# Graph network on one core: filter input on ScalarE's queue, ScalarE compares for four tiles, aggregation by source half

## The chip, the cores and the metric

One core of a Trainium2 chip. The metric is device time in microseconds of one execution.

## What is computed

256 nodes with 512 features, 4352 edges sorted by target. Two residual layers on x:

```python
# layer 0: normalised dense adjacency, applied to a linear map
h = relu(layernorm(x))
adj[src, dst] = 1; adj[dst, src] = 1; adj += eye
adj = adj * dinv[:, None] * dinv[None, :]          # dinv = deg ** -0.5
x = x + adj @ (h @ W0) + bias0
# layer 1: edge filters, gather, tensor products, scatter
h = relu(layernorm(x))
hs, hv = h[:, :128] @ w_in2f_s, h[:, 128:] @ w_in2f_v      # 32 channels, scalar and 3-vector
s, v = hs[dst], hv[dst]
Wf = (softplus_shifted(edge_attr_20 @ W1 + b1) @ W2 + b2) * edge_weight
edge = products of s, v, edge_attr_4 and Wf
agg = segment_sum(edge, src)
x = x + output_net(agg)
```

(dst and src stand here in the roles of idx_j and idx_i; only the products that reach the output are needed.)

## The kernel before

The 4352 edges are 34 tiles of 128; a group is four tiles, so there are nine groups (the last of two tiles). Every engine has its own program, and the order in each is written out by hand; semaphores join them.

Compares. VectorE builds one-hot matrices Os and Od [128 edges, 256 nodes] in bf16 for each tile, in seven waves (WAVES, function onehots, line 406): an is_equal of iota_r with the edges' ids for Os and another for Od. Od lies in the memory of WQ, which gets its own data later (so rows on line 412 call it WQ). TensorE counts the edges between nodes with Os and Od (adjacency, line 601) into banks 4 and 5, and from that VectorE makes CI (line 454), TensorE transposes it (line 666, called CT here) and VectorE makes A and the degrees (line 465), degve (line 469) and GpSimd the two scales by a power (line 354, scales(1) first).

Layer 0. VectorE does the statistics of x (lines 431 to 437) and h1, TensorE transposes h1 (line 625), ScalarE copies the result out (h1T, line 214), and TensorE multiplies by W0 in four k blocks for each half of the nodes (first_layer, line 629). The product is scaled and split into two parts, hW_hi on ScalarE (line 251) and hW_lo on VectorE (line 479). A times these gives L0 (line 674), in the order hi of both halves, then lo of both. x1 (line 485) is L0 times dinv plus xb, where xb = x + bias0 (line 472, VectorE).

Filter net. TensorE makes z from the filter input f_sb and w1 (hidden, line 611, three pieces). ScalarE takes Abs of each (line 207), then Exp (218) and Ln (221) of all, VectorE adds the positive part into za (line 446), ScalarE rounds hX and hY (231, 232), VectorE takes the rests hXlo (449) and hYlo (475). The output weights are split into w2_hi (ScalarE, 216) and w2_lo (VectorE, 442), the bias row into b2p on GpSimd (lines 341 to 347). filters(g) (line 636) multiplies group by group.

Layer 1. After x1 come h2, its transposes (line 688) and node channels (695), which end in HL (277, 504). Node one-hots OdT [128 nodes, 4352 edges], two halves of the nodes (a = 0, 1) and four chunks of the edges, are compares with dst_bc: on VectorE (node_onehots, line 459) chunks 0 and 1 of both halves, on GpSimd (node_onehots_late, line 358) chunks 3 and 2 of half 0, on ScalarE (lines 244 and 247) chunks 2 and 3 of half 1, as 1 minus distance. The loop over the groups (gather 721, VectorE 514 to 565, ScalarE 301, 305, 240, 284, 268, GpSimd 378, 395, 399, scatter 733) and the tail follow.

Loads. SP's queue issues idx, x, f, w0, dst, bias0, then small ones; ScalarE's queue w1, w2, b2, yr. xb lies in the memory of f_sb.

## Time and profile before

| | |
|---|---|
| median of 3 runs | 71.96 us (71.57, 71.96, 72.97) |
| profiled execution | 71.83 us, its span 69.8 us |
| TensorE matmul busy | 61.7 us (88%), granted clock 0.988 of full |
| VectorE busy | 60.1 us (86%) |
| ScalarE busy | 48.6 us (70%) |
| GpSimd busy | 39.5 us (57%) |
| DMA | 5.65 MB, nearly all of the loads before 16.5 us |

All times below are microseconds from the start of the span. An engine that is not busy for a moment matters only where something on the last chain waits for it.

### The profile page before, as it was taken

Reading aid. Unit: us, or ns where it says so; the run is one execution under the profiler, and the core shown is the slowest. Engines: PE = TensorE matmul, PEld = TensorE weight load, DVE = VectorE, ACT = ScalarE, POOL = GpSimd, SP = SyncE. Lnnn points to the kernel's source line nnn. Section 1 sums busy time; section 2 is a strip of 40 time slices with the busy share of each in tenths; the row PEclk is TensorE's granted clock in tenths of the full one; section 3 lists DMA queues with packets and bytes.
Section 4 is the critical chain, followed back from the end, with each engine's and each line's share of the span. In section 5 each row is a group of like instructions: output and inputs, shape, how many; then the busy total and the mean of one; then the engine's idle time right before and its main releaser. Section 6 shows DMA issues by size and latency. Waiting matters only on the chain.

```text
span 69.8 us, 1215 instructions
## 1 busy us (share of the span) xinstructions
PE 61.7 (88%) x407; PEld 48.6 (70%) x407; DVE 60.1 (86%) x124; ACT 48.6 (70%) x74; POOL 39.5 (57%) x46
## 2 busy tenths in 40 slices
PE   3999998999999999897998979999999999998340
PEld 1236754568834268796987969998898989997220
DVE  4599999999979968989999898989898999972760
ACT  0700059978999697967979999988696969732700
POOL 5000030000676989594799979999999988700000
PEclk9999999999999999999999999999999999999995
DMA  0899998984000000000000000000000000000044
GB/s 1 129 396 247 361 499 379 449 317 124 9 0 0 0 0 0 0 0 5 0 0 0 0 0 9 5 0 0 0 0 0 0 0 9 0 0 0 0 148 153
DMA packets 3049, 5.65 MB, mean 81 GB/s; under 512 B 540, under 2 KB 1936, under 8 KB 2916
## 3 DMA queue, kind: packets, MB, share of 16 engines
q1 hardware_dynamic: 2274, 5.14, 21.3%
q10 hardware_dynamic: 770, 0.44, 2.2%
q8 instruction: 3, 0.05, 0.3%
q14 instruction: 2, 0.02, 0.1%
HBM read 5.06 MB, written 0.52 MB: 80 GB/s over the span
## 4 chain that ended last, share of the span: by engine, by line
DVE 45%; PE 20%; issue 14%; ACT 13%; DMA 3%; DVEq 0%; ACTq 0%
ACT OsR L240 8%; DVE WQ L412 7%; DVE Os L412 7%; PE pair L632 5%; ACT w_sb L284 5%; DVE dst_bc L565 4%; PE pair L733 4%; PE pair L742 4%; DVE pair L514 3%; PE pair L674 3%; DMA idx_sb<-idx 3%; PE pair L721 3%; DVE w_sb L485 2%; DVE za L446 2%; DVE hX L449 2%
## 5 line engine op out<-in xcount | busy, mean ns | idle before, releaser
L733 PE MATMUL pair<-OsR,Mh 128*128 128x256 f32 x56 | 13.6, 281 | 0.0
L733 PE MATMUL pair<-OsR,Ml 128*128 128x256 f32 x56 | 13.6, 281 | 0.0
L721 PE MATMUL pair<-HL,OdT 128*128 128x256 f32 x68 | 10.1, 289 | 1.6 <-DVE dst_bc L565 0.7
L395 POOL TENSOR_TENSOR Ml<-dst_bc,Mh 128x512 fp32r<-128x512 f32 x8 | 10.4, 1305 | 1.1 <-ACT Mh L301 1.0
L721 PEld LDWEIGHTS pair<-HL,OdT 128*128 128x128 f32 x68 | 8.6, 188 | 2.8 <-issue 2.8
L733 PEld LDWEIGHTS pair<-OsR,Ml 128*128 128x128 f32 x56 | 10.5, 188 | 0.0
L733 PEld LDWEIGHTS pair<-OsR,Mh 128*128 128x128 f32 x56 | 10.5, 188 | 0.0
L605 PEld LDWEIGHTS pair<-WQ,Os 128*128 128x128 bf16 x68 | 6.8, 104 | 4.0 <-DVE WQ L412 1.8
L605 PE MATMUL pair<-WQ,Os 128*128 128x256 bf16 x68 | 9.4, 297 | 0.2 <-DVE WQ L412 0.2
L399 POOL TENSOR_TENSOR Ml<-dst_bc,Mh 128x512 fp32r<-128x512 f32 x7 | 9.2, 1309 | 0.0
L240 ACT ACTIVATE OsR<-Os 128x1024 fp32r<-128x1024 bf16 (+1 forms) x9 | 9.0, 999 | 0.0
L632 PE MATMUL pair<-w_sb,h1T 128*128 128x512 f32 x16 | 7.7, 601 | 0.3 <-ACT h1T L214 0.3
L305 ACT ACTIVATE Mh<-dst_bc 128x512 fp32r<-128x512 f32 (+1 forms) x9 | 5.5, 609 | 3.1 <-DVE dst_bc L565 3.0
L514 DVE TENSOR_TENSOR pair<-pair,w_sb 128x512 f32<-128x512 f32 (+1 forms) x10 | 6.2, 619 | 1.3 <-ACT w_sb L284 1.2
L358 POOL TENSOR_SCALAR OdT<-dst_bc,iota_c 128x1088 fp32r<-128x1088 int32 x2 | 6.1, 3054 | 1.6 <-DVE OdT L459 1.4
L341 POOL CAST b2p<-b_sb 96x128 bf16<-96x128 f32 x1 | 1.4, 1402 | 8.3 <-issue 8.3
L534 DVE TENSOR_TENSOR pair<-pair,WQ 128x512 f32<-128x512 f32 (+1 forms) x9 | 6.0, 662 | 0.1
L378 POOL TENSOR_TENSOR WQ<-WQ,y 128x256 f32<-128x256 f32 (+1 forms) x9 | 5.8, 652 | 0.1
L207 ACT ACTIVATE za<-pair 128x512 f32<-128x512 f32 (+1 forms) x3 | 1.4, 489 | 6.3 <-PE pair L613 6.3
L284 ACT ACTIVATE w_sb<-pair 128x512 f32<-128x512 f32 (+1 forms) x10 | 5.2, 518 | 0.8 <-PE pair L721 0.7
L412 DVE TENSOR_TENSOR Os<-iota_r,idp 128x512 bf16<-128x512 bf16 (+3 forms) x7 | 5.6, 796 | 0.0
L412 DVE TENSOR_TENSOR WQ<-iota_r,idp 128x512 bf16<-128x512 bf16 (+3 forms) x7 | 5.6, 796 | 0.0
(122 smaller groups left out, 140.2 us busy)
## 6 DMA issues: line engine op xcount, KB each, us to landing
dst_bc<-dst_row SPq DMA_DIRECT2D x1, 2176.0 KB, 12.9
w_sb<-w SPq DMA_DIRECT2D x1, 1024.0 KB, 8.1
x_sb<-x SPq DMA_DIRECT2D x1, 512.0 KB, 4.4
out<-x_sb SPq DMA_DIRECT2D x2, 192.0 KB, 1.9
f_sb<-f_t SPq DMA_DIRECT2D x1, 378.0 KB
b_sb<-bias SPq DMA_DIRECT2D x1, 256.0 KB, 13.1
w_sb<-w ACTq DMA_DIRECT2D x1, 128.0 KB, 4.1
out<-x_sb ACTq DMA_DIRECT2D x1, 128.0 KB, 1.9
```

Of the source, the lines that this page charges most:

```text
L240: nc.scalar.activation(OsR[:, g % RG, 0:n, :], Os[:, t0:t0 + n, :], ACT.Copy).then_inc(q["OsR"], 1)
L284: nc.scalar.activation(G_lo[:, g % RS, j0:j1, :, :], rows_of(g)[:, j0:j1, 1, :, :], ACT.Copy).then_inc(q["Glo"], 1)
L358: nc.gpsimd.tensor_scalar(OdT[:, 0, c * E // 4:(c + 1) * E // 4], dst_bc[:, c * E // 4:(c + 1) * E // 4], iota_c[:, 0:1], None, ALU.is_equ ...
L395: nc.gpsimd.tensor_tensor(Ml[:, o, 0:n, feats(1)], M[:, o, 0:n, feats(1)], Mh[:, o, 0:n, feats(1)].bitcast(fp32), ALU.subtract).then_inc(q ...
L399: nc.gpsimd.tensor_tensor(Ml[:, o, 0:n, feats(0)], M[:, o, 0:n, feats(0)], Mh[:, o, 0:n, feats(0)].bitcast(fp32), ALU.subtract).then_inc(q ...
L412: last = nc.vector.tensor_tensor(into[:, t0:t1, :].rearrange("p t (h k) -> p t h k", k=2), nodes, of_edge, ALU.is_equal)
L514: nc.vector.tensor_tensor(hi, hi, G_lo[:, g % RS, j0:j1, :, :].rearrange("p t c f -> p t (c f)"), ALU.add).then_inc(q["add"], 1)
L534: nc.vector.tensor_tensor(L, G, wq[:, :, 3:7, :], ALU.mult).then_inc(q["Q"], 1)
L605: last = nc.tensor.matmul(bank[4 + a][:, 0:N], Os[:, t, a * P:(a + 1) * P], Od[:, t, :], start=(t == 0), stop=(t == T - 1))
L632: last = nc.tensor.matmul(bank[a][:, :], h1T[:, a, k, :], w0_sb[:, k, :], start=(k == 0), stop=(k == KD - 1))
L721: last = nc.tensor.matmul(gpair[g % 2][:, j * 2 * C:(j + 1) * 2 * C], OdT[:, a, t * P:(t + 1) * P], HL[:, a, :, :], start=(a == 0), stop=( ...
L733: last = nc.tensor.matmul(bank[4 + b][:, 0:N], part[:, g % RG, j, feats(b)], OsR[:, g % RG, j, :], start=(TG * g + j == 0 and part is Mh), ...
```

## The change

- The filter input f_t is loaded first on ScalarE's queue instead of third on SP's. The hidden products are put between the adjacency products of early waves; the waves become (0,2) (2,4) (4,8) (8,12) (12,20) (20,28) (28,30).
- The one-hots of tiles 30 to 33 are made on ScalarE: eight Abs of iota_r minus the id (negidx) and two Relu of one minus the distance. Their adjacency products stand between the transposes of the two halves of h1.
- b2p is made of two parts in fp32r instead of three in bf16: a copy on ScalarE, a difference on GpSimd.
- xb moves from VectorE to GpSimd, ahead of scales. hYlo is done in three pieces. w2_lo goes behind the last wave.
- Node one-hots: ScalarE keeps chunk 2 of half 1, VectorE takes chunk 3 of half 1 and does chunk 0 of half 0 between the two hW_lo; GpSimd does chunk 2, then 3, of half 0. The scratch of ScalarE's (gap) lies in h1.
- A times hW goes by half: hi and lo of half 0, then of half 1. One k block of the second half of the first layer goes ahead of CT.
- y_blocks(0, free) goes ahead of ScalarE's node one-hot, wc_sb's copy ahead of h2.

```diff
     WARM = 6
-    WAVES = ((0, 2), (2, 6), (6, 12), (12, 20), (20, 28), (28, 32), (32, T))
+    TA = 4
+    TV = T - TA
+    WAVES = ((0, 2), (2, 4), (4, 8), (8, 12), (12, 20), (20, 28), (28, TV))
     LN_EPS = 1e-5
...
             sp.dma_start(x_sb[:, :, :], x.rearrange("(a p) d -> p a d", p=P)).then_inc(d_x, 16)
-            sp.dma_start(f_sb[0:KF, :], f_t).then_inc(d_f, 16)
             sp.dma_start(w0_sb[:, :, :], w0.rearrange("(k p) n -> p k n", p=P)).then_inc(d_w0, 16)
...
+            act.dma_start(f_sb[0:KF, :], f_t).then_inc(d_f, 16)
             act.dma_start(w1_sb[:], w1).then_inc(d_w1, 16)
...
+            act.wait_ge(d_idx, 16)
+            nc.scalar.activation(negidx[:, :, :], idx_sb[:, :].rearrange("p (h t) -> p h t", h=2)[:, :, TV:T], ACT.Copy,
+                                 scale=-1.0).then_inc(q["negidx"], 1)
+            act.wait_ge(q["negidx"], 1)
+            act.wait_ge(q["iota"], 1)
+            act.wait_ge(q["half"], 3)
+            for h, into in enumerate((Os, Od)):
+                for i in range(TA):
+                    nc.scalar.activation(dist[:, h, i, :], iota_r[:], ACT.Abs, bias=negidx[:, h, i:i + 1]).then_inc(q["dist"], 1)
+                act.wait_ge(q["dist"], TA * (h + 1))
+                nc.scalar.activation(into[:, TV:T, :], dist[:, h, :, :], ACT.Relu, bias=one[:, 0:1],
+                                     scale=-1.0).then_inc(q["near"], 1)
             absolute(0)
...
                 nc.scalar.activation(h1T[:, a, :, :], bank[(6, 1)[a]][:, :], ACT.Copy).then_inc(q["h1T"], 1)
+            act.wait_ge(d_b2, 16)
+            nc.scalar.activation(b2p[:], b2_sb[:], ACT.Copy).then_inc(q["b2p"], 1)
             act.wait_ge(d_w2, 16)
...
                 t0, n = TG * g, tiles(g)
-                act.wait_ge(q["onehot"], wave(t0 + n - 1))
+                act.wait_ge(q["onehot"], wave(min(t0 + n, TV) - 1))
+                if t0 + n > TV:
+                    act.wait_ge(q["near"], 2)
                 if g >= RG:
...
-            act.wait_ge(d_dst, 16)
-            act.wait_ge(q["negc"], 1)
-            nc.scalar.activation(gap, dst_bc[:, E // 2:], ACT.Abs, bias=iota_n[:, 1:2]).then_inc(q["gap"], 1)
-            act.wait_ge(q["gap"], 1)
-            act.wait_ge(q["half"], 3)
-            nc.scalar.activation(OdT[:, 1, E // 2:], gap, ACT.Relu, bias=one[:, 0:1], scale=-1.0).then_inc(q["OdTa"], 1)
-            act.wait_ge(q["scales"], 1)
-            for a in range(NH):
-                act.wait_ge(q["hW"], a + 1)
-                nc.scalar.activation(hW_hi[:, a, :], bank[a][:, :], ACT.Copy, scale=s1[:, a:a + 1]).then_inc(q["hW_hi"], 1)
-            act.wait_ge(q["OdTa"], 1)
+            act.wait_ge(q["near"], 2)
             act.wait_ge(q["adj"], 1)
...
             y_blocks(0, free)
+            act.wait_ge(d_dst, 16)
+            act.wait_ge(q["negc"], 1)
+            act.wait_ge(q["tp1"], NH)
+            nc.scalar.activation(gap, dst_bc[:, E // 2:3 * E // 4], ACT.Abs, bias=iota_n[:, 1:2]).then_inc(q["gap"], 1)
+            act.wait_ge(q["scales"], 1)
+            for a in range(NH):
+                act.wait_ge(q["hW"], a + 1)
+                nc.scalar.activation(hW_hi[:, a, :], bank[a][:, :], ACT.Copy, scale=s1[:, a:a + 1]).then_inc(q["hW_hi"], 1)
+            act.wait_ge(q["gap"], 1)
+            nc.scalar.activation(OdT[:, 1, E // 2:3 * E // 4], gap, ACT.Relu, bias=one[:, 0:1],
+                                 scale=-1.0).then_inc(q["OdTa"], 1)
+            act.wait_ge(q["wc"], 1)
+            nc.scalar.activation(wc_sb[:], bank[1][:, 0:B], ACT.Copy, scale=SF * SB).then_inc(q["wcs"], 1)
+            act.wait_ge(q["OdTa"], 1)
             act.wait_ge(q["x1"], 1)
...
                 filters_out(g)
-            act.wait_ge(q["wc"], 1)
-            nc.scalar.activation(wc_sb[:], bank[1][:, 0:B], ACT.Copy, scale=SF * SB).then_inc(q["wcs"], 1)
             act.wait_ge(q["s2"], 1)
...
             nc.gpsimd.memset(one[:], 1.0).then_inc(q["half"], 1)
-            nc.gpsimd.memset(ones[:], 1.0).then_inc(q["ones"], 1)
+            nc.gpsimd.memset(ones[:].bitcast(i32), 0x3f800000).then_inc(q["ones"], 1)
...
-            pool.wait_ge(q["onehot"], len(WAVES))
-            pool.wait_ge(d_b2, 16)
-            nc.gpsimd.tensor_copy(b2p[:], b2_sb[:]).then_inc(q["b2p"], 1)
             pool.wait_ge(q["b2p"], 1)
-            nc.gpsimd.tensor_tensor(b2r[:], b2_sb[0:64, :], b2p[0:64, :], ALU.subtract).then_inc(q["b2r"], 1)
-            pool.wait_ge(q["b2r"], 1)
-            nc.gpsimd.tensor_copy(b2p[0:64, :], b2r[:]).then_inc(q["b2p"], 1)
+            nc.gpsimd.tensor_tensor(b2p[32:64, :], b2_sb[32:64, :], b2p[32:64, :].bitcast(fp32), ALU.subtract).then_inc(q["b2p"], 1)
             pool.wait_ge(q["b2p"], 2)
-            nc.gpsimd.tensor_tensor(b2p[0:32, :], b2r[0:32, :], b2p[0:32, :], ALU.subtract).then_inc(q["b2p"], 1)
-            pool.wait_ge(q["b2p"], 3)
+            pool.wait_ge(d_x, 16)
+            pool.wait_ge(d_b0, 16)
+            pool.wait_ge(q["z"], 3)
+            nc.gpsimd.tensor_tensor(xb[:, :, :], x_sb[:, :, :], b0_sb[:].unsqueeze(1).broadcast_to((P, NH, D)),
+                                    ALU.add).then_inc(q["xb"], 1)
             pool.wait_ge(q["degve"], 1)
...
             pool.wait_ge(q["scales"], 2)
-            node_onehots_late(3)
+            node_onehots_late(2)
             pool.wait_ge(q["OdTp"], 1)
...
             scaled_late(1)
-            pool.wait_ge(q["OdT"], 4)
-            node_onehots_late(2)
+            node_onehots_late(3)
             scaled_late(2)
...
             onehots(2)
+            onehots(3)
...
             nc.vector.tensor_scalar(ve[:], mv1[:, :, 1], LN_EPS, None, ALU.add).then_inc(q["ve"], 1)
-            for w in range(3, len(WAVES)):
+            for w in range(4, len(WAVES)):
                 onehots(w)
-                if w == 4:
-                    dve.wait_ge(q["w2hi"], 1)
-                    nc.vector.tensor_tensor(w2_lo[:], w2_sb[:], w2_hi[:].bitcast(fp32), ALU.subtract).then_inc(q["w2lo"], 1)
+                if w == 5:
                     dve.wait_ge(q["zln"], 1)
...
                                                        ALU.max, ALU.add).then_inc(q["hT"], 1)
+            dve.wait_ge(q["w2hi"], 1)
+            nc.vector.tensor_tensor(w2_lo[:], w2_sb[:], w2_hi[:].bitcast(fp32), ALU.subtract).then_inc(q["w2lo"], 1)
             dve.wait_ge(q["hhi"], 1)
...
-            dve.wait_ge(d_b0, 16)
-            nc.vector.tensor_tensor(xb[:, :, :], x_sb[:, :, :], b0_sb[:].unsqueeze(1).broadcast_to((P, NH, D)),
-                                    ALU.add).then_inc(q["xb"], 1)
             dve.wait_ge(q["hhi"], 2)
-            nc.vector.tensor_tensor(hY[0:64, :], za[64:128, :], hY[64:128, :].bitcast(fp32), ALU.subtract).then_inc(q["hYlo"], 1)
+            for c in range(3):
+                cols = slice(c * NG * P // 3, (c + 1) * NG * P // 3)
+                nc.vector.tensor_tensor(hY[0:64, cols], za[64:128, cols], hY[64:128, cols].bitcast(fp32),
+                                        ALU.subtract).then_inc(q["hYlo"], 1)
             dve.wait_ge(q["scales"], 1)
+            dve.wait_ge(d_dst, 16)
             for a in range(NH):
...
                                                hW_hi[:, a, :].bitcast(fp32), ALU.mult, ALU.subtract).then_inc(q["hW_lo"], 1)
+                if a == 0:
+                    node_onehots(0, 0)
             dve.wait_ge(q["scales"], 2)
...
             dve.wait_ge(q["x1"], 2)
+            dve.wait_ge(q["OdTa"], 1)
             nc.vector.tensor_scalar(h2[:, 1, :], x1[:, 1, :], float(D), xsum[:, 1:2], ALU.mult,
...
                                     ALU.max).then_inc(q["h2T"], 1)
-            dve.wait_ge(d_dst, 16)
-            for a in range(NH):
-                node_onehots(a, 0)
+            node_onehots(1, 0)
+            node_onehots(0, 1)
             dve.wait_ge(q["s2"], 1)
...
                                                HL[:, a, 0, :].bitcast(fp32), ALU.mult, ALU.subtract).then_inc(q["Hl"], 1)
-            for a in range(NH):
-                node_onehots(a, 1)
+            node_onehots(1, 1)
+            node_onehots(1, 3)
...
                     dve.wait_ge(q["OdT"], 4)
-                    dve.wait_ge(q["OdTp"], 2)
+                    dve.wait_ge(q["OdTp"], 1)
+                    dve.wait_ge(q["OdTa"], 1)
                 dve.wait_ge(q["add"], g + 2)
...
                 for t in ts:
-                    pe.wait_ge(q["onehot"], wave(t))
+                    if t < TV:
+                        pe.wait_ge(q["onehot"], wave(t))
+                    else:
+                        pe.wait_ge(q["near"], 2)
                     for a in range(NH):
                         last = nc.tensor.matmul(bank[4 + a][:, 0:N], Os[:, t, a * P:(a + 1) * P], Od[:, t, :],
-                                                start=(t == 0), stop=(t == T - 1))
-                if t == T - 1:
+                                                start=(t == 0), stop=(t == TV - 1))
+                if t == TV - 1:
                     last.then_inc(q["adj"], 1)
...
-            adjacency(range(2, 6))
-            adjacency(range(6, 12))
-            pe.wait_ge(d_f, 16)
-            pe.wait_ge(d_w1, 16)
-            for c in range(3):
-                hidden(c)
-            pe.wait_ge(q["eye"], NH + 1)
-            for a in range(NH):
+            def transposed(a):
+                pe.wait_ge(q["eye"], NH + 1)
                 pe.wait_ge(q["h1"], a + 1)
...
                 last.then_inc(q["tp1"], 1)
+            adjacency(range(2, 4))
+            pe.wait_ge(d_f, 16)
+            pe.wait_ge(d_w1, 16)
+            hidden(0)
+            hidden(1)
+            adjacency(range(4, 8))
+            hidden(2)
+            adjacency(range(8, 12))
+            transposed(0)
+            adjacency(range(TV, T))
+            transposed(1)
             pe.wait_ge(d_w0, 16)
...
             first_layer(0, 2, 3)
-            adjacency(range(20, T))
+            adjacency(range(20, TV))
             first_layer(0, 3, KD)
+            first_layer(1, 0, 1)
...
             last.then_inc(q["CT"], 1)
-            first_layer(1, 0, KD)
-            for p, (part, ready) in enumerate(((hW_hi, "hW_hi"), (hW_lo, "hW_lo"))):
-                for b in range(NH):
+            first_layer(1, 1, KD)
+            for b in range(NH):
+                for p, (part, ready) in enumerate(((hW_hi, "hW_hi"), (hW_lo, "hW_lo"))):
                     pe.wait_ge(q[ready], b + 1)
...
```

## Rows read from the trace of the kernel before

**Rows 1.** The page, chain that ended last, by engine.
```profile
DVE 45%; PE 20%; issue 14%; ACT 13%; DMA 3%; DVEq 0%; ACTq 0%
```
**Rows 2.** Timeline, VectorE: start us, us, engine, line, operation, count, idle before.
```profile
2.76 0.23 DVE L423 CAST idp<-idx_sb 128x136 bf16<-128x136 int32 x1 [0.71 <-DMA idx_sb<-idx]
...
9.32 0.38 DVE L437 TENSOR_SCALAR ve<-mv 128x2 f32<-128x2 f32 x1
9.62 1.21 DVE L412 TENSOR_TENSOR Os<-iota_r,idp 128x2048 bf16<-128x2048 bf16 x1
...
14.16 0.41 DVE L442 TENSOR_TENSOR w_lo<-w_sb,w_hi 128x256 fp32r<-128x256 f32 x1
14.49 1.47 DVE L446 SCALAR_TENSOR_TENSOR za<-pair,za 128x512 f32<-128x512 f32 x3
...
17.87 1.35 DVE L449 TENSOR_TENSOR hX<-za,hX 64x1152 fp32r<-64x1152 f32 x1
19.25 0.76 DVE L454 SCALAR_TENSOR_TENSOR warmup<-pair,eye_sb 128x256 bf16<-128x256 f32 x2
...
21.31 0.16 DVE L469 TENSOR_TENSOR deg<-deg,ve 128x2 f32<-128x2 f32 x1
21.39 1.22 DVE L472 TENSOR_TENSOR f_sb<-x_sb,b_sb 128x1024 f32<-128x1024 f32 x1
...
24.03 1.44 DVE L479 SCALAR_TENSOR_TENSOR hW_lo<-pair,scales,hW_hi 128x512 fp32r<-128x512 f32 x2
26.31 0.75 DVE L485 SCALAR_TENSOR_TENSOR w_sb<-pair,scales,f_sb 128x512 f32<-128x512 f32 x1 [0.84 <-PE pair L674]
...
29.71 1.47 DVE L459 TENSOR_SCALAR OdT<-dst_bc,iota_c 128x1088 fp32r<-128x1088 int32 x2
```
**Rows 3.** Timeline, ScalarE.
```profile
10.68 1.08 ACT L214 ACTIVATE h1T<-pair 128x512 f32<-128x512 f32 x2
11.65 0.42 ACT L216 ACTIVATE w_hi<-w_sb 128x256 fp32r<-128x256 f32 x1
...
13.15 1.25 ACT L221 ACTIVATE za<-za,warm 128x1152 f32<-128x1152 f32 x1
...
23.22 1.46 ACT L251 ACTIVATE hW_hi<-pair,scales 128x512 fp32r<-128x512 f32 x2 [0.60 <-POOL scales L354]
```
**Rows 4.** Timeline, TensorE matmuls (CT is line 666).
```profile
8.10 2.10 PE L613 MATMUL pair<-f_sb,w_sb 84*128 84x512 f32 x6
10.04 1.04 PE L625 MATMUL pair<-id_sb,h 128*128 128x128 f32 x8
11.42 1.95 PE L632 MATMUL pair<-w_sb,h1T 128*128 128x512 f32 x4 [0.34 <-ACT h1T L214]
13.21 1.91 PE L605 MATMUL pair<-WQ,Os 128*128 128x256 bf16 x16
...
20.07 0.40 PE L666 MATMUL pair<-eye_sb,warmup 128*128 128x128 bf16 x4 [0.17 <-DVE warmup L454]
```
**Rows 5.** Timeline, GpSimd (y, b2p, the first scales).
```profile
9.05 0.62 POOL L335 TENSOR_TENSOR y<-yr_sb 128x136 f32<-128x136 f32 x1 [7.54 <-DMA yr_sb<-yr]
17.97 1.40 POOL L341 CAST b2p<-b_sb 96x128 bf16<-96x128 f32 x1 [8.29 <-issue]
...
21.61 1.58 POOL L354 TENSOR_TENSOR scales<-deg,neghalf 128x2 f32<-128x2 f32 x1 [0.89 <-POOL b2p L347]
```
**Rows 6.** The page, costliest groups: busy us, mean ns, idle before.
```profile
L395 POOL TENSOR_TENSOR Ml<-dst_bc,Mh 128x512 fp32r<-128x512 f32 x8 | 10.4, 1305 | 1.1 <-ACT Mh L301 1.0
```
**Rows 7.** The bias row's load: its issue in SP's timeline, and its landing time.
```profile
3.15 0.44 SPq L184 DMA_DIRECT2D b_sb<-bias  x1
b_sb<-bias SPq DMA_DIRECT2D x1, 256.0 KB, 13.1
```
**Rows 8.** Windows: PE, PEld, DVE, ACT, POOL busy, PEclk, DMA share, GB/s.
```profile
0.00:5.60 5.60, 4.26 (x13) 1.60 (x14) 3.83 (x11) 1.28 (x1) 0.88 (x10) 1.00 0.67 182
37.10:56.50 19.40, 18.30 (x145) 17.32 (x144) 18.20 (x38) 17.16 (x28) 18.77 (x20) 1.00 0.00 1
```

34 lines of the change are left out of this document (19 added, 15 removed).

## The prediction

> **What bounds the kernel now.** I read the page first (busy shares, then the chain that ended last), then the chain in order of time, then the timeline of each engine up to 37 us, and last the DMA issues. VectorE has the largest part of the chain, 45% [rows 1]. The span has three stretches. From 0 to about 26 us the graph is prepared: compares, adjacency, first layer, aggregation. From 26 to 37 us come the second norm and the filters. From 37 us nine groups of edges run through a loop. Six passes take the 19.4 us of one window, 3.2 each, with VectorE busy for 18.2 and ScalarE for 17.2 of it [rows 8]. The diff leaves every instruction of the loop and of the tail in place, so I carry both over unchanged. What counts is when x1 (line 485) starts, now at 26.31 [rows 2]: all behind it follows from it, and the sum is a sum of shifts of that one moment.
>
> Up to there two engines share the limit. VectorE has no gap of note from 2.76 to 20.0 [rows 2]. TensorE is held by compares until the hidden products start at 8.10 and has almost no break from there to the transposes of CI (CT) at 20.07 [rows 4].
>
> **The change, part by part.**
> *Filter input first.* idx, x, the filter input f (378 KB) and w1 are 0.97 MB together. Up to 5.6 us the DMA engines moved 182 GB/s, which is 1.02 MB [rows 8]. So I let f and w1 be there at 5.6 (bounds 5.0 and 6.2). The hidden products stood at 8.10; TensorE gets work for its early gap.
>
> *TensorE up to the transposes of h1.* From 5.6: hidden products 1.94 in all (8.10 to 10.04), three blocks of eight adjacency products at 0.88 (16 take 1.91 with the last one's run-out, so 0.11 each), transposes 0.9. That ends at 5.6 + 5.5 = 11.1. Before it was 11.08 [rows 4]. The early start is spent, because the products of the four ScalarE tiles now stand ahead of the second transposes.
>
> *ScalarE.* Eight Abs of 256 elements, at most 0.42 each as w2_hi took, two casts of 1024 at about 1.0 and three Abs of z (1.4) fill 3.4 to at most 10.6, where ScalarE was mostly idle. Then comes a queue that nothing hides: second h1T copy at 11.2, 0.5; b2p copy 0.2 (new here); w2_hi, Exp and Ln 2.75 (11.65 to 14.40) [rows 3]. Ln ends at 14.7 instead of 14.40.
>
> *VectorE.* Four tiles fewer save 8 x 0.14 = 1.1 us (a compare of eight tiles takes 1.21), the extra early wave adds 0.14, and w2_lo (0.33) goes behind. VectorE would reach za (line 446) at 14.3, but za waits for Ln: 14.75 to 16.15, before 14.49 to 15.89. The last wave is now two tiles (2 x 0.33), then w2_lo 0.33, then hXlo, which waits for ScalarE's hX: 17.4. Left alone, hXlo would run 17.45 to 18.8 and CI (line 454) start at 18.83, 0.4 sooner than 19.25 [rows 2]. TensorE agrees: from 11.1, two k blocks 1.79 (11.42 to 13.21), 16 products 1.75, a block 0.87, 20 products 2.2, two blocks 1.74 give 19.45; CT comes at 19.65, behind CI, in place of 20.07 [rows 4].
>
> *xb moves to GpSimd (line 472).* This is the term that decides. VectorE took 1.22 us for it. On GpSimd the nearest row is a tensor_tensor of 512 fp32 elements, 1.305 us [rows 6], so 2.6 for 1024. It waits for the bias row, which lands at 3.15 + 13.1 = 16.25 [rows 7], and it reads SBUF, as do VectorE's instructions of just that time: the last wave, w2_lo and hXlo have two SBUF operands each. The trace shows that such pairs exclude each other. GpSimd's cast b2p took 1.40 us, from 17.97 to 19.37, for 128 elements, while VectorE's hX ran 17.87 to 19.22 [rows 2, 5]. The first scales took 1.58 for two elements beside VectorE's xb, which ended at 22.61. The other way round, VectorE's ve (line 437, two elements) took 0.38 where degve took 0.16, and ended at 9.70, just after GpSimd's y at 9.67. So I take full exclusion: GpSimd gets in at 16.25 or at the next instruction's end (16.5), mean 16.35, and keeps VectorE's two-operand work out until 18.95. Then the rest of the last wave 0.45 on average, w2_lo 0.33, hXlo 1.37: CI at 21.1, 1.85 later than before. The other bound is no exclusion: CI at 18.83.
>
> The Trainium skill says the same of this pair ("SBUF — State Buffer", Who interferes with whom): a VectorE instruction with two SBUF inputs contends with a GpSimd instruction that reads SBUF, and whoever starts first keeps the shared ports for the whole instruction. The rows above agree, but in none of them does a long GpSimd instruction hold VectorE.
>
> *From CI to x1.* CI to the end of degve takes 2.2 (19.25 to 21.47), as before. Then the move pays. The first scales ended 1.7 after degve because xb stood in front; now only a third of hYlo (0.5) does, and it is ready after 1.1. hW_hi and hW_lo are 0.7 each [rows 2, 3]. Between the two hW_lo stands a node one-hot of 0.7 (two take 1.47). The second hW_hi is ready 0.7 after the first, so the one-hot costs its 0.7 in front of the second hW_lo, which is the last that x1 waits for. Exclusion case: degve ends 23.3, scales 24.4, first hW_hi 25.1, first hW_lo 25.8, one-hot 26.5, second hW_lo 27.2, x1 0.55 later (two products): 27.75, +1.45. Without exclusion: 21.05, 22.15, 22.9, 23.6, 24.35, 25.1, x1 25.7: -0.6. In both, TensorE's first layer (CT + 3.0: 24.9 or 22.65) is just in time. The order by source half is worth nothing by itself, as the last wait is the second hW_lo in both orders.
>
> *The rest, at nothing.* ScalarE's node one-hots halve, and VectorE gains a chunk but does chunk (0,0) ahead of x1, so from x1 to the first rows_sum it has four chunks in both kernels. The wc copy goes ahead of h2, into idle time of ScalarE; without that cover it costs 0.3. GpSimd's late one-hot need not wait for OdT and GpSimd starts its loop 1 to 2 us sooner, but the loop does not wait for it. The bias product in 64 rows of fp32r streams as many columns; if its weight load is slower it shows 0.1 before the transposes of h2.
>
> **Sum.** Profiled execution 71.83 (span 69.8 and 2.0 around it) + 1.45 = 73.3. That execution stands 0.13 below the median of 71.96; I make no correction.
>
> **The rivals.**
> *1. No exclusion, or GpSimd yields between pieces.* For it: no row shows a long GpSimd instruction holding VectorE, and ve is a tiny case. Against: the pairs above that met did exclude. 71.83 - 0.6 = 71.2, faster than before. It decides when VectorE is held for less than about 0.8 us.
> *2. idx comes late.* Its load has been beside w1 (rows of 512 B); now it is beside the 4.6 KB rows of f. VectorE's start at 2.76 hangs on it [rows 2]. Up to 0.4 is absorbed, as za waits for Ln anyhow. If it is 1.4 late and nothing excludes: 71.2 + 1.0 = 72.2; with exclusion the two overlap in part, about 73.8. The Trainium skill has each DMA engine take turns between queues packet by packet ("DMA: Bandwidth & Descriptors", Queues, rings and completion order). No row here shows what a large packet does to a small one beside it.
> *3. More gain than I see.* f at 5.0 takes 0.4 off Ln; then VectorE limits, za at 14.3, x1 at 25.2; without exclusion 70.7. To pass 2% (70.5) the loop would have to gain as well.
>
> **Chances and range.** Exclusion 0.50, no exclusion 0.30, idx late 0.10, more gain 0.10. About 2% (1.4 us) is what a measurement of this kernel can tell from no change. The exclusion case straddles that bound: 0.28 of its 0.50 goes to slower, the rest to within. idx late gives 0.04 to slower, more gain 0.08 to faster. So faster 0.08, within 0.60, slower 0.32. The likeliest case has 72.7 to 73.9 as its own range (the bias row or GpSimd 0.6 sooner at best, 0.6 of idx on top at worst). With both signs the range is 70.9 to 73.9.
>
> **What the profile after would show.** xb on GpSimd near 16.3 to 19 and the last wave or hXlo on VectorE stretched or ending late, near 21: forecast right. hXlo ending near 18.8 beside a running xb: rival 1. idp starting after 3.2: rival 2. Hidden products at about 5.6, Ln ending near 14.7, scales 1.1 after degve, the second hW_lo as the last release of x1, and six loop passes in 19.3 us test the other steps. The prediction is wrong if the bias row lands after 17.5 (xb would then lie beside CI and A, which read PSUM), or if the loop's period moves: 0.1 there is 0.8 in the end.

## The result: 78.5 us, 7% slower

| | before | changed |
|---|---|---|
| median | 71.79 us (4 runs, 71.57 to 72.97) | 78.48 us (4 runs, 76.62 to 79.91) |
| profiled execution, its span | 71.83, 69.8 us | 79.89, 77.8 us |
| TensorE's mean granted clock | 0.988 | 0.920 |

The ratio is 1.072, interval 1.069 to 1.076. The forecast was 73.3, range 70.9 to 73.9: it is wrong, outside the range. In some executions of the changed kernel TensorE's clock is low for one or two stretches; the ratio leaves them out, and the profile below is of one with two such stretches.

The page of the changed kernel: the rows of TensorE and of its granted clock over 40 slices, then the chain that ended last, by engine and by line.

```profile
PE   3909999999999976989999999999999999998630
...
PEclk9998555899999999999758999999999999999995
...
PE 64%; DVE 13%; ACT 7%; DMA 5%; issue 5%; POOL 1%; DVEq 0%
PE pair L769 17%; PE pair L757 13%; PE pair L684 8%; PE pair L631 6%; DMA idx_sb<-idx 5%; PE pair L681 5%; PE pair L639 5%; PE pair L778 3%; PE pair L728 2%; DVE za L463 2%; DVE hW_lo L499 2%; ACT za L238 2%; DVE OdT L478 2%; ACT hX L248 2%; POOL scales L373 1%
```

In place of VectorE with 45% [rows 1], TensorE has 64% of the chain. Four of the entries were not among the fifteen largest before: the filter products (L684), the adjacency products (L631), the bias product (L681) and the hidden products (L639). The load of idx has gone from 3% to 5%. The clock row has a hole at about 8 to 14 us and another at 38 to 41.

VectorE's timeline of the changed kernel up to x1 (start, length, line, operation, idle before it and its releaser):

```profile
4.86 0.23 DVE L441 CAST idp<-idx_sb 128x136 bf16<-128x136 int32 x1 [2.81 <-DMA idx_sb<-idx]
...
19.52 1.49 DVE L463 SCALAR_TENSOR_TENSOR za<-pair,za 128x512 f32<-128x512 f32 x3 [3.27 <-ACT za L238]
...
23.62 0.76 DVE L473 SCALAR_TENSOR_TENSOR warmup<-pair,eye_sb 128x256 bf16<-128x256 f32 x2
...
25.68 0.16 DVE L488 TENSOR_TENSOR deg<-deg,ve 128x2 f32<-128x2 f32 x1
...
27.89 0.75 DVE L499 SCALAR_TENSOR_TENSOR hW_lo<-pair,scales,hW_hi 128x512 fp32r<-128x512 f32 x1 [0.51 <-ACT hW_hi L272]
28.55 1.30 DVE L478 TENSOR_SCALAR OdT<-dst_bc,iota_c 128x1088 fp32r<-128x1088 int32 x1
29.78 0.74 DVE L499 SCALAR_TENSOR_TENSOR hW_lo<-pair,scales,hW_hi 128x512 fp32r<-128x512 f32 x1
31.21 0.75 DVE L507 SCALAR_TENSOR_TENSOR w_sb<-pair,scales,f_sb 128x512 f32<-128x512 f32 x1 [0.69 <-PE pair L707]
```

Against [rows 2]: idp starts at 4.86 in place of 2.76, VectorE then waits 3.27 us for Ln, CI (the row called warmup) starts at 23.62 in place of 19.25, x1 at 31.21 in place of 26.31. The node one-hot between the two hW_lo takes 1.30, where one of a pair took 0.74.

TensorE's and GpSimd's timelines of the same stretch, and two windows (TensorE, loads of weights, VectorE, ScalarE, GpSimd busy, granted clock, DMA):

```profile
5.94 1.28 PE L631 MATMUL pair<-WQ,Os 128*128 128x256 bf16 x8 [2.03 <-DVE WQ L430]
7.06 3.35 PE L639 MATMUL pair<-f_sb,w_sb 84*128 84x512 f32 x4
...
31.46 0.50 PE L681 MATMUL pair<-b2p,ones 64*128 64x512 f32 x1
31.88 0.38 PE L684 MATMUL pair<-w_hi,hX 128*128 128x256 f32 x1
...
32.55 0.50 PE L681 MATMUL pair<-b2p,ones 64*128 64x512 f32 x1
```
```profile
17.52 2.36 POOL L367 TENSOR_TENSOR f_sb<-x_sb,b_sb 128x1024 f32<-128x1024 f32 x1
```
```profile
8.00:14.00 6.00, 6.00 (x21) 3.34 (x20) 5.86 (x12) 3.98 (x8) 0.68 (x1) 0.50 1.08 438
...
38.00:42.00 4.00, 4.00 (x18) 3.34 (x19) 3.75 (x6) 1.78 (x5) 3.82 (x2) 0.57 0.00 0
```

TensorE waits 2.03 us for the first compares, and from 8 to 14 us it runs at the granted clock 0.50, the 1.2 GHz level. Four hidden products (1024 of the 1152 columns) take 3.35, where all six took 2.10 [rows 4]. A filter group takes 1.09 (31.46 to 32.55). xb runs 17.52 to 19.88, while VectorE is idle, waiting for Ln: in this execution the predicted exclusion has almost nothing to hold (za, which follows at 19.52, reads PSUM and takes 1.49, against 1.47 before).

### One table for all kernels

Each span is cut at three VectorE instructions: CI, x1, and the first product MA of the loop (MA0, line 565 before). All are starts in the profiled execution.

| kernel | idp | CI | x1 | x1 to MA0 | MA0 to end | span |
|---|---|---|---|---|---|---|
| before | 2.76 | 19.25 | 26.31 | 10.85 | 32.64 | 69.8 |
| changed (two low clocks) | 4.86 | 23.62 | 31.21 | 12.77 | 33.82 | 77.8 |
| 1 changed, again (no low grant) | 4.65 | 21.54 | 29.12 | 12.05 | 33.13 | 74.3 |
| 2 before, f first on ScalarE | 4.68 | 21.42 | 28.46 | 10.88 | 32.56 | 71.9 |
| 5 changed, more warm-up | 4.79 | 21.13 | 28.70 | 12.17 | 33.03 | 73.9 |
| 7 changed, f on SP, bias bf16 | 2.65 | 21.11 | 28.68 | 11.49 | 32.63 | 72.8 |
| 8 before, xb on GpSimd | 2.62 | 21.25 | 28.38 | 10.86 | 32.96 | 72.2 |
| 9 as 7, xb on VectorE | 2.63 | 19.14 | 27.39 | 11.78 | 32.63 | 71.8 |
| 11 before, ScalarE's one-hots | 2.64 | 18.43 | 25.48 | 10.85 | 32.57 | 68.9 |

### The profile page after: what moved, and what is told of

It is laid out like the page before. It is cut to its first block, busy times and chain, and to the rows that moved or that the text cites. A ratio compares the mean times of both kernels' runs of the same rounds, so it can differ in the third digit from the quotient of the medians.

```text
span 77.8 us, 1235 instructions
## 1 busy us (share of the span) xinstructions
PE 68.3 (88%) x407; PEld 51.6 (66%) x407; DVE 60.2 (77%) x126; ACT 53.0 (68%) x86; POOL 39.4 (51%) x44
## 4 chain that ended last, share of the span: by engine, by line
PE 64%; DVE 13%; ACT 7%; DMA 5%; issue 5%; POOL 1%; DVEq 0%
PE pair L769 17%; PE pair L757 13%; PE pair L684 8%; PE pair L631 6%; DMA idx_sb<-idx 5%; PE pair L681 5%; PE pair L639 5%; PE pair L778 3%; PE pair L728 2%; DVE za L463 2%; DVE hW_lo L499 2%; ACT za L238 2%; DVE OdT L478 2%; ACT hX L248 2%; POOL scales L373 1%
## 5 line engine op out<-in xcount | busy, mean ns | idle before, releaser
L631 PE MATMUL pair<-WQ,Os 128*128 128x256 bf16 x68 | 10.3, 308 | 2.1 <-DVE WQ L430 2.0
L631 PEld LDWEIGHTS pair<-WQ,Os 128*128 128x128 bf16 x68 | 7.3, 110 | 6.9 <-DVE WQ L430 3.8
L757 PE MATMUL pair<-HL,OdT 128*128 128x256 f32 x68 | 10.7, 303 | 0.4
L757 PEld LDWEIGHTS pair<-HL,OdT 128*128 128x128 f32 x68 | 9.4, 203 | 1.2 <-issue 1.1
L326 ACT ACTIVATE Mh<-dst_bc 128x512 fp32r<-128x512 f32 (+1 forms) x9 | 5.5, 608 | 3.0 <-DVE dst_bc L588 2.8
L377 POOL TENSOR_SCALAR OdT<-dst_bc,iota_c 128x1088 fp32r<-128x1088 int32 x2 | 6.7, 3350 | 0.2 <-POOL scales L373 0.2
L397 POOL TENSOR_TENSOR WQ<-WQ,y 128x256 f32<-128x256 f32 (+1 forms) x9 | 6.3, 703 | 0.4 <-ACT WQ L291 0.4
L291 ACT ACTIVATE WQ<-pair 128x512 f32<-128x512 f32 (+1 forms) x9 | 5.0, 570 | 1.4 <-PE pair L684 1.4
L478 DVE TENSOR_SCALAR OdT<-dst_bc,iota_c 128x1088 fp32r<-128x1088 int32 x5 | 5.5, 1124 | 0.0
L322 ACT ACTIVATE Mh<-dst_bc 128x512 fp32r<-128x512 f32 (+1 forms) x9 | 5.4, 600 | 0.0
L430 DVE TENSOR_TENSOR Os<-iota_r,idp 128x512 bf16<-128x512 bf16 (+2 forms) x7 | 5.1, 724 | 0.0
```

The lines of the kernel that those rows point to most:

```text
L377: nc.gpsimd.tensor_scalar(OdT[:, 0, c * E // 4:(c + 1) * E // 4], dst_bc[:, c * E // 4:(c + 1) * E // 4], iota_c[:, 0:1], None, ALU.is_equ ...
L397: nc.gpsimd.tensor_tensor(WQ[:, t0:t0 + n, 0:2, :], WQ[:, t0:t0 + n, 0:2, :], y[:, t0:t0 + n, 0:1].unsqueeze(3).broadcast_to((P, n, 2, F)) ...
L478: nc.vector.tensor_scalar(OdT[:, a, lo:hi], dst_bc[:, lo:hi], iota_c[:, a:a + 1], None, ALU.is_equal).then_inc(q["OdT"], 1)
L631: last = nc.tensor.matmul(bank[4 + a][:, 0:N], Os[:, t, a * P:(a + 1) * P], Od[:, t, :], start=(t == 0), stop=(t == TV - 1))
L757: last = nc.tensor.matmul(gpair[g % 2][:, j * 2 * C:(j + 1) * 2 * C], OdT[:, a, t * P:(t + 1) * P], HL[:, a, :, :], start=(a == 0), stop=( ...
```

## The experiments

### 1 to 4: how much of it is the late index load?

The first theory (A): idx, held back beside f's load, carries most of the loss. Its rival (B): the fp32r bias product. 1 is the changed kernel once more.

> The changed kernel again, beside the other three on one chip. Its runs so far were 76.62, 77.08, 79.89 and 79.91, with mean granted clock 0.999, 0.974, 0.92 and 0.978. Both theories expect a ratio to the kernel before of 1.07 and idx landing near 4.85. If the spread belongs to the clock of TensorE, a run at clock 0.999 must be near 76.6.

Measured 78.99 (76.29 to 82.31), the profiled one 76.29. Even here, with a granted clock of 1.00, eight adjacency products of the first stretch take 1.89 us (timeline of TensorE; behind 10 us eight take 1.04). The granted clock reads 1.00 ahead of the wait as well, where the six warm-up products take 2.74 us, 0.46 each for 512 columns, so it doesn't show this half rate:

```profile
5.73 1.89 PE L631 MATMUL pair<-WQ,Os 128*128 128x256 bf16 x8 [1.82 <-DVE WQ L430]
7.41 2.80 PE L639 MATMUL pair<-f_sb,w_sb 84*128 84x512 f32 x4
10.05 1.04 PE L631 MATMUL pair<-WQ,Os 128*128 128x256 bf16 x8
```

2 is the kernel before with f first on ScalarE's queue, and nothing else.

```diff
-            sp.dma_start(f_sb[0:KF, :], f_t).then_inc(d_f, 16)
...
+            act.dma_start(f_sb[0:KF, :], f_t).then_inc(d_f, 16)
             act.dma_start(w1_sb[:], w1).then_inc(d_w1, 16)
```

> The kernel before, with one edit: the filter input is loaded first on ScalarE's queue. Theory A (idx is held up by the 4.6 KB rows of f beside it, and that carries most of the loss): idx lands near 4.85 in place of 2.75, all of VectorE's compares start 2.1 later, total +2.1 to +4 (74 to 76), the more the more TensorE's clock drops after its gap. Theory B (idx late by chance or by the order inside the new kernel; the loss is the fp32r bias product): idx near 2.75 and 71.8.

Measured 74.0 (73.78 to 74.07), ratio 1.029 (1.026 to 1.033). idp starts 1.92 later, CI by 2.17 and x1 by 2.15:

```profile
4.68 0.23 DVE L423 CAST idp<-idx_sb 128x136 bf16<-128x136 int32 x1 [2.62 <-DMA idx_sb<-idx]
```

The index load (34 KB) lands 4.1 us after its issue in the changed kernel, 3.9 in 2 and 2.0 before. That is the term that I had given a chance of 0.10, alone worth 2.2 us. Whether f's long rows or its bytes hold idx back, no run separates. TensorE waits 1.84 us here too, but with 24 adjacency products ahead of the hidden ones these take 2.10 as before.

3 is the changed kernel with f back on SP (third), its hidden products still ahead.

```diff
+            sp.dma_start(f_sb[0:KF, :], f_t).then_inc(d_f, 16)
             sp.dma_start(w0_sb[:, :, :], w0.rearrange("(k p) n -> p k n", p=P)).then_inc(d_w0, 16)
...
-            act.dma_start(f_sb[0:KF, :], f_t).then_inc(d_f, 16)
```

> The changed kernel with the filter input back as SP's third load, all else kept. Theory A: idx lands at 2.75, no gap of TensorE after its warm-up longer than before, total 72 to 74 (2.1 of idx and 0.5 to 2 of half clock come back; hidden products may wait for f near 6.6). Theory B: 76 or more stays, as the nine bias products at 1.1 instead of 0.7 per group stay.

Measured 79.89 (77.46 to 80.77): not faster, theory A fell as it stood. idp is back at 2.67, but now TensorE's fixed order has it wait for f, and behind the wait it is slow (its timeline; all six had taken 2.10):

```profile
7.47 3.78 PE L639 MATMUL pair<-f_sb,w_sb 84*128 84x512 f32 x4 [1.82 <-DMA f_sb<-f_t]
```

4 is the changed kernel with the bias product in three bf16 parts on 96 rows, as before.

```diff
-        ones = sb("ones", [64, P], fp32r)
-        b2p = sb("b2p", [64, P], fp32r)
+        ones = sb("ones", [96, P], bf16)
+        b2p = sb("b2p", [96, P], bf16)
```

> The changed kernel with the bias product as before (three bf16 parts in 96 rows), its first copy still on ScalarE, the rest on GpSimd at the new place. The profile after shows 1.09 us per filter group against 0.70 before. Theory B: 0.4 for each group that lies on the chain, the two before the transposes of h2 and some of the next five, -1.5 to -2.5, so 74 to 75. Theory A: -0.8 at most (only the two groups ahead of the transposes of h2 are on the chain), about 75.8; idx stays near 4.85.

Measured 77.6 (76.81 to 78.97), ratio 1.070 (1.065 to 1.076) beside the change's 1.072, which is neither theory's time. The scatter of the early stretch covers the term: inconclusive, and settled by 6 and 7.

### 5: fill TensorE's wait

The new theory (C): TensorE's wait near 4 to 6 us is followed by products at half rate, and this is a large part. 5 is the changed kernel with eleven warm-up products in place of six.

```diff
-    WARM = 6
+    WARM = 11
```

> The changed kernel with eleven warm-up products in place of six; nothing else is new. The five more (about 0.43 us each at half rate) lie in TensorE's wait for the one-hots, 3.9 to 5.9 us. Theory C, TensorE's rate: after that wait its products run at half rate (256 columns in 0.23 us in place of 0.11) and this carries a large part of the loss; filled, the hidden products should take about 2 us for six in place of 2.8 to 3.4 for four, Ln should end near 15.5 in place of 17.4 (fast run) or 19.5, and the time come to 75 to 76.5. Theory D, the late start alone (idp at 4.7 in place of 2.8) and the bias product: the rate does not matter, the time stays at 77 to 79.

Measured 76.17 (75.95 to 77.52), ratio 1.061 (1.058 to 1.065). The wait is gone and so is the half rate behind it (TensorE's timeline):

```profile
5.87 1.28 PE L631 MATMUL pair<-WQ,Os 128*128 128x256 bf16 x8
6.99 1.91 PE L639 MATMUL pair<-f_sb,w_sb 84*128 84x512 f32 x4
8.73 1.04 PE L631 MATMUL pair<-WQ,Os 128*128 128x256 bf16 x8
```

Four hidden products take 1.91 in place of 3.35 or 2.80, and the median falls by 2.3 us, almost all of it scatter: the best runs of the changed kernel (76.3 to 76.6) are only 0.3 to 0.7 slower. C holds for what lies above 76.6, not for the other 4 us: in 5 Ln ends at 16.09, where it ended at 17.40 in 1 and at 19.49 in the changed kernel's profile. This kernel is the clean case of the change, span 73.9, 4.1 over before: 2.39 ahead of x1, 1.32 from there to MA0, 0.39 behind.

### 6 and 7: f undisturbed, then the bias product

6 is 3 with the hidden products back behind the adjacency products of tiles 4 to 11; 7 is 6 with the bias as in 4.

```diff
             adjacency(range(2, 4))
+            adjacency(range(4, 8))
+            adjacency(range(8, 12))
             pe.wait_ge(d_f, 16)
             pe.wait_ge(d_w1, 16)
             hidden(0)
             hidden(1)
-            adjacency(range(4, 8))
             hidden(2)
-            adjacency(range(8, 12))
```

> The changed kernel with f back on SP's queue (third) and the hidden products back behind the adjacency products of tiles 4 to 11, so that neither the compares nor TensorE wait for a load longer than before. What is left of the change is ScalarE's one-hots, xb on GpSimd, the fp32r bias row, the node one-hots in another order, aggregation by half. Theory C: with no wait of TensorE ahead of f, the half rate until about 14 us that the version with f on SP alone still had goes; za is at about 15, x1 at about 27, and with the bias product at +0.4 per group the time is 73 to 75. Theory E, the rest of the change (one-hots on GpSimd beside VectorE's, fp32r bias) carries most: 76 or more, with x1 near 27 and the loss behind it.

> As the kernel with f on SP and late hidden products, but the bias product in three bf16 parts on 96 rows, as before (the first copy stays on ScalarE). The difference of the two is the price of the fp32r form. The trace of the changed kernel shows a filter group at 1.09 us against 0.70 before, two of them ahead of the loop and one in each pass. If TensorE bounds the end: 0.4 for each of the first two and up to 0.4 a pass, 1 to 3 us less. If VectorE bounds the loop: 0.4 to 0.8 less, the two groups ahead of it. My prediction had it at nothing.

6: 75.94 (75.79 to 79.0), ratio 1.058 (1.054 to 1.062). 7: 75.15 (75.06 to 75.23), ratio 1.048 (1.045 to 1.050). So the fp32r form of the bias product costs 0.8 us. In the table, between 5 and 7, x1 to MA0 falls by 0.68 (the filters of two groups stand ahead of the transposes of h2) and the rest by 0.40, and the loop is then at 32.63, before 32.64. That is 1.1 of span; 0.2 of it comes back outside the span, where 5 has 2.05 us and 7 has 2.26. The profiled execution of 6 isn't in the table: in it TensorE waited 1.31 us for f, and CI started at 22.75.

And 6 is only 0.2 below 5. Undoing the late idx gained 2.1 us at idp and nothing at CI (21.11 in 7, against 21.13 in 5). What had taken its place is the next experiment's subject.

### 8 and 9: xb on GpSimd

8 is the kernel before with xb alone moved, ahead of GpSimd's bias work. 9 is 7 with xb back on VectorE behind degve.

```diff
+            pool.wait_ge(d_x, 16)
+            pool.wait_ge(d_b0, 16)
+            pool.wait_ge(q["z"], 3)
+            nc.gpsimd.tensor_tensor(xb[:, :, :], x_sb[:, :, :], b0_sb[:].unsqueeze(1).broadcast_to((P, NH, D)),
+                                    ALU.add).then_inc(q["xb"], 1)
             pool.wait_ge(q["onehot"], len(WAVES))
```

> The kernel before with one step alone: xb on GpSimd, from about 16.3 us, ahead of its bias work, beside VectorE's last compare waves, the first piece of the rests (hXlo) and nothing idle. Theory of the prediction, full exclusion: VectorE is held for up to 2.4 us, CI starts near 21.2 in place of 19.25, and with xb's 1.2 us gone from VectorE behind it the time is 72.5 to 73.5. Rival, sharing: VectorE's instructions beside it run at most a little longer (0.4 us in all), CI near 19.5, the time 71 to 71.8.

> The last kernel (f on SP, hidden products late, bias in bf16) with xb back on VectorE at its old place, behind degve. In the kernel before, xb on GpSimd alone cost 2.4 us, and there a compare that takes 0.41 took 2.58 beside it. If that exclusion is the whole of it here too, CI starts at 19.0 to 19.4 in place of 21.11, the first scales are again 1.7 behind degve, x1 starts near 27.2 in place of 28.7, and the time is 73.2 to 73.8. If the late CI had another cause (ScalarE's longer queue, TensorE), CI stays after 20.5 and the time over 74.5.

8: 74.19 (74.01 to 74.44), ratio 1.035 (1.031 to 1.038). VectorE's timeline, then GpSimd's:

```profile
16.93 2.58 DVE L417 TENSOR_TENSOR Os<-iota_r,idp 128x512 bf16<-128x512 bf16 x1
19.43 0.41 DVE L417 TENSOR_TENSOR WQ<-iota_r,idp 128x512 bf16<-128x512 bf16 x1
```
```profile
16.59 2.63 POOL L342 TENSOR_TENSOR f_sb<-x_sb,b_sb 128x1024 f32<-128x1024 f32 x1 [7.41 <-DMA b_sb<-bias]
```

A compare that takes 0.41 took 2.58, and it ended 0.29 after xb did: GpSimd held VectorE for 2.17 us. CI moved by 2.00. The exclusion of the forecast is shown, with its length. The time is above the 72.5 to 73.5 expected, because the move paid nothing back: CI to x1 took 7.13, before 7.06. The first hW_hi started 2.01 behind degve's end (25.48 against 23.47), beside the whole hYlo of 1.35. 9: 73.79 (73.76 to 74.69), ratio 1.032 (1.024 to 1.040), with CI at 19.14. In 7, where a compare took 2.57 beside xb, xb on GpSimd thus costs 1.4 us. 1.3 of it stands at x1: 1.97 at CI, less 0.68 from there (7.57 against 8.25).

In 5, where idx is late, it holds less, because xb started beside za (VectorE's timeline, then GpSimd's):

```profile
16.37 1.47 DVE L463 SCALAR_TENSOR_TENSOR za<-pair,za 128x512 f32<-128x512 f32 x3
17.77 1.27 DVE L430 TENSOR_TENSOR Os<-iota_r,idp 128x512 bf16<-128x512 bf16 x1
```
```profile
16.40 2.36 POOL L367 TENSOR_TENSOR f_sb<-x_sb,b_sb 128x1024 f32<-128x1024 f32 x1 [2.17 <-DMA b_sb<-bias]
```

za reads one operand from PSUM, took 1.47 as in [rows 2], and was not held. The compare behind it lost 0.86. Another compare, at 13.83, took 1.48 in place of 1.22 beside GpSimd's difference for b2p.

### 10 and 16: another order on VectorE, and TensorE's clock

10 is the kernel before with hYlo in three pieces first, then xb in halves, one of them in VectorE's wait ahead of x1.

```diff
-            nc.vector.tensor_tensor(xb[:, :, :], x_sb[:, :, :], b0_sb[:].unsqueeze(1).broadcast_to((P, NH, D)),
-                                    ALU.add).then_inc(q["xb"], 1)
...
+            nc.vector.tensor_tensor(xb[:, 0, :], x_sb[:, 0, :], b0_sb[:], ALU.add).then_inc(q["xb"], 1)
             dve.wait_ge(q["scales"], 1)
...
+            nc.vector.tensor_tensor(xb[:, 1, :], x_sb[:, 1, :], b0_sb[:], ALU.add).then_inc(q["xb"], 1)
             dve.wait_ge(q["scales"], 2)
```

> The kernel before, still with xb on VectorE, in another order there: hYlo in three pieces first, then half 0 of xb, then the two hW_lo, then half 1 of xb, where VectorE waited 0.84 us for the aggregation. GpSimd's first scales then meet a VectorE piece of 0.5 us in place of xb's 1.2. If TensorE's first layer (its second half ends near 24) bounds hW_hi, x1 moves by 0.1 to 0.3 and the time is 71.4 to 71.7. If VectorE bounds, x1 moves by 0.5 and the time is 71.2.

Measured 73.49 (73.45 to 74.85), ratio 1.024 (1.022 to 1.027): slower than either guess, with x1 at 26.27 as before. TensorE's first gather and four windows:

```profile
32.70 1.82 PE L724 MATMUL pair<-HL,OdT 128*128 128x256 f32 x8 [0.71 <-DVE HL L507]
```
```profile
32.00:33.00 1.00, 0.30 (x2) 0.33 (x3) 1.00 (x3) 0.65 (x1) 0.40 (x1) 0.99 0.00 0
33.00:34.00 1.00, 1.00 (x7) 1.00 (x6) 0.83 (x2) 0.30 (x1) 0.07 (x1) 0.50 0.00 0
34.00:35.00 1.00, 1.00 (x6) 0.82 (x6) 0.43 (x1) 0.53 (x3) 1.00 (x1) 0.50 0.00 0
35.00:36.00 1.00, 1.00 (x6) 1.00 (x6) 0.87 (x2) 0.56 (x2) 1.00 (x1) 0.50 0.00 0
```

VectorE's first pair of node one-hots started 0.37 later (30.08 against 29.71) and took 1.84 in place of 1.47, beside GpSimd's scaled_late. So HL came 0.40 later, TensorE waited 0.71, and from 33 us its clock stood at 0.50. 16 puts three products without use there.

```diff
             filters(2)
+            for _ in range(3):
+                nc.tensor.matmul(bank[0][:, :], warmup[:, 0:P], warmup[:], start=True, stop=True)
```

> The kernel with xb in halves on VectorE, which took 73.5 although its x1 started where that of the kernel before did: TensorE waited 0.71 us ahead of the first gather (0.36 before) and then ran at the lower clock (0.50 of full) from 33 to 36.5. Here three products without use (0.22 each) fill that wait. If the wait brings the low clock, it goes, and the time is 71.5 to 72.0. If the stretch has another cause, the clock falls all the same and the time stays at 73.4 or more.

Measured 72.34 (72.09 to 73.31), ratio 1.008 (1.005 to 1.011), 1.15 less than 10, if 0.1 to 0.3 above the 71.5 to 72.0 expected. The first gather takes 1.18, and the windows from 32 to 38 read 0.95 throughout, with no stretch at 0.50:

```profile
32.98 1.18 PE L726 MATMUL pair<-HL,OdT 128*128 128x256 f32 x8
```

So in this kernel the low clock came with TensorE's wait and went when it was filled. The wait alone doesn't bring it each time. In 9 TensorE waited as long at the same place, and its clock read 1.00 from 33 to 38 us:

```profile
33.84 1.19 PE L759 MATMUL pair<-HL,OdT 128*128 128x256 f32 x8 [0.70 <-DVE HL L528]
```

(Another run of 9, at 74.69, has a mean clock of 0.966.) What else decides isn't shown. For the changed kernel's second hole, at 38 us, not even the wait is there: TensorE waited less than 0.3 us ahead of that gather. Its cause stays open.

### 14, 17: GpSimd's second node one-hot

14 and 17 are one kernel: 9, with GpSimd's one-hot of chunk 3 again behind all of VectorE's.

```diff
+            pool.wait_ge(q["OdT"], 5)
             node_onehots_late(3)
```

> The kernel with xb back on VectorE, and GpSimd's second node one-hot again waiting until VectorE's are done, as in the kernel before. In the last one the two pairs of VectorE's one-hots took 1.84 and 2.31 where they had taken 1.47 and 1.54, beside GpSimd's scaled_late and its one-hot. If the sharing is the cause, the second pair takes 1.5 again, the first w2y starts 0.7 sooner and the time is 72.9 to 73.2. If something else of that stretch is (the order of copies on ScalarE, the wait for HL), the time stays at 73.6 to 73.9.

> The kernel with GpSimd's second node one-hot waiting for VectorE's, once more, since its profiled execution could not be read. As before: 72.9 to 73.2 with the second pair of VectorE's one-hots at 1.5 if the sharing is the cause of the longer pair (2.31), 73.6 to 73.9 if it is not. A third way it can go: GpSimd's later work makes TensorE wait longer ahead of the loop, and its clock falls; then about 74.7.

14 took 73.45, 74.71 and 74.79, and 203.81 in its profiled execution. 17: 74.06 (73.29 to 76.19), ratio 1.021 (1.016 to 1.027) against 1.032 of 9. VectorE's second pair in 9, then in 17:

```profile
33.50 2.31 DVE L477 TENSOR_SCALAR OdT<-dst_bc,iota_c 128x1088 fp32r<-128x1088 int32 x2
```
```profile
33.55 1.47 DVE L478 TENSOR_SCALAR OdT<-dst_bc,iota_c 128x1088 fp32r<-128x1088 int32 x2
```

GpSimd's one-hot beside it costs the pair 0.84 us. The runs at 73.29 and 73.41 are 0.4 to 0.5 below 9, where 0.6 to 0.9 was expected. In the profiled execution (74.7) the third way of the expectation came: TensorE waited 0.71 ahead of the first gather and its clock fell to 0.50. The run at 76.19 has no trace; its mean clock is lower still, 0.932. The pair is shown as a cause; how much of it a kernel keeps depends on what the clock does there.

### 12 and 18: why the bias product takes 0.43 us

12 is the changed kernel with three forms of the product by group; 18 is 6 with it on 128 rows, half of them zero.

```diff
+                if g % 3 == 1:
+                    nc.tensor.matmul(ps, ones[:], b2w[:, 0:n * P], start=True, stop=False)
+                elif g % 3 == 2:
+                    for i in range(n // 2):
+                        nc.tensor.matmul(ps[:, 2 * P * i:2 * P * (i + 1)], ones[:], b2w[:, 0:2 * P], start=(i == 0), stop=False)
```
```diff
-        b2p = sb("b2p", [64, P], fp32r)
+        b2p = sb("b2p", [P, P], fp32r)
```

> The changed kernel with its fp32r bias product in three forms by group: groups 0, 3, 6 as it is (the 128 bias columns repeated four times by a broadcast, one product of 512), groups 1, 4, 7 from a row written out to 512 columns, groups 2, 5, 8 as two products of 256 columns from it. The broadcast product takes 0.43 us; 256 columns of another fp32r product take 0.11. If the repeated operand is the cause, the written out form takes 0.22. If the 64 rows or the width of 512 is the cause, it takes 0.43 too, and the two of 256 tell whether the width is.

> The version with f on SP, late hidden products and the fp32r bias product (75.9), with that product on 128 rows, of which rows 64 to 127 are zero. Written out or in two halves it stayed at 0.43 us. If the 64 rows are the cause, it takes 0.22 and the time is 75.1 to 75.4, as with the bf16 form; if not, 0.43 and 75.8 to 76.0, and what makes an fp32r product of constants slower stays open.

12 (one execution, 76.48): TensorE's timeline, each form and the product behind it.

```profile
29.50 0.50 PE L691 MATMUL pair<-b2p,ones 64*128 64x512 f32 x1
29.93 0.39 PE L694 MATMUL pair<-w_hi,hX 128*128 128x256 f32 x1
...
30.60 0.50 PE L686 MATMUL pair<-b2w,ones 64*128 64x512 f32 x1
31.03 0.39 PE L694 MATMUL pair<-w_hi,hX 128*128 128x256 f32 x1
...
34.87 0.50 PE L689 MATMUL pair<-b2w,ones 64*128 64x256 f32 x2
35.30 0.39 PE L694 MATMUL pair<-w_hi,hX 128*128 128x256 f32 x1
```

All three take 0.43 from start to start. On 128 rows (18):

```profile
29.89 0.40 PE L681 MATMUL pair<-b2p,ones 128*128 128x512 f32 x1
30.12 0.28 PE L684 MATMUL pair<-w_hi,hX 128*128 128x256 f32 x1
```

0.23, and a group goes from 1.09 to 0.78 (bf16: 0.70). The 64 rows are the cause; why 64 rows cost more isn't shown. 18 took 75.41 (74.83 to 75.63, and one execution of 101.28), its ratio 1.045 (1.038 to 1.051), against 1.058 of 6.

### 11 and 15: ScalarE's one-hots alone

11 is the kernel before with ScalarE's compares for tiles 30 to 33, the waves up to tile 30, their adjacency products behind the transposes of h1, and w2_lo behind the last wave. 15 also moves w2_hi behind Ln.

```diff
-    WAVES = ((0, 2), (2, 6), (6, 12), (12, 20), (20, 28), (28, 32), (32, T))
+    TA = 4
+    TV = T - TA
+    WAVES = ((0, 2), (2, 6), (6, 12), (12, 20), (20, 28), (28, TV))
...
+                    nc.scalar.activation(dist[:, h, i, :], iota_r[:], ACT.Abs, bias=negidx[:, h, i:i + 1]).then_inc(q["dist"], 1)
...
+            adjacency(range(TV, T))
             pe.wait_ge(d_w0, 16)
```

> The kernel before with ScalarE's one-hots for four tiles alone: waves up to tile 30, their adjacency products behind the transposes of h1, w2_lo behind the last wave. VectorE has 1.1 us less before hXlo, ScalarE 6 us more while it waited. If VectorE was what bounds CI: CI near 18.6, the time 71.0 to 71.4. If TensorE is as full as VectorE (almost no break from 8.1 to CT) or ScalarE's queue up to Ln and hX takes its place: CI within 0.2 of 19.25 and the time 71.6 to 72.0.

> The kernel before with ScalarE's one-hots, the version that was faster than before (71.06), with w2_hi moved behind Ln: VectorE waited 0.21 for Ln and 0.23 for hX, and w2_hi (0.3) stands ahead of Exp. If ScalarE bounds there: CI 0.2 to 0.3 sooner, 70.8. If TensorE, which goes into the transposes of CI without a pause, bounds: nothing, 71.0 to 71.2.

11: 71.06 (70.89 to 72.22), ratio 0.992 (0.989 to 0.995); CI at 18.43, x1 at 25.48. 15: 70.94 (70.89 to 70.97), ratio 0.989 (0.988 to 0.991). VectorE's timeline of 15 at CI:

```profile
18.37 0.76 DVE L473 SCALAR_TENSOR_TENSOR warmup<-pair,eye_sb 128x256 bf16<-128x256 f32 x2 [0.28 <-PE pair L627]
```

VectorE now waits for TensorE there, so the rest of ScalarE's 0.3 is lost. This one part of the change, without the others, is 0.7 us faster than the kernel before (1%, clear of noise but under 2%).

## Why the prediction was wrong, step by step

Three steps failed. idx was left on time in the main case, and it came 2.1 us late. TensorE's products were all charged at full rate. And what lies from x1 on was put at nothing, where 5 has 1.7 us more. The term called decisive, the exclusion, was right in kind and size, but in the changed kernel's profile it wasn't what cost the time.

**The filter input at 5.6 and the rival "idx late".** That f comes early was right, or at least nothing waited for it: the first hidden product ran at 7.06. What it displaces was mis-sized: 1.9 to 2.1 us at idp in place of the 1.4 of that rival, at a chance of 0.10. The sentence on turns between queues had no row behind it, and I let that make it improbable. The rule ("DMA: Bandwidth & Descriptors", Queues, rings and completion order, in the Trainium skill) pointed the right way: the 34 KB of idx, beside f on the other queue, landed 4.1 us after the issue in place of 2.0.

**TensorE up to the transposes of h1, end at 11.1.** It was 12.6 in 5 and 16.0 in the changed kernel. Of the 1.5 us in 5, 1.4 are the late idx: the hidden products stand behind eight adjacency products and start at 6.99, not at 5.6. The rest is rate. I charged every product at its full rate, but behind a wait of 1.8 to 2.0 us four hidden products took 2.80 and 3.35, against 1.91 in 5: 0.9 to 1.4 more. In none of my rivals did the order put a wait ahead of work, though [rows 4] shows TensorE's early work as dependent on each wave.

**Ln at 14.7.** 19.5 in the changed kernel, 17.4 in 1, 16.1 in 5. It follows from the two above: in 7 and 9, without either, Ln ended at 15.0.

**xb on GpSimd excludes VectorE.** The mechanism is shown in 8, 7 and 9: 2.0 us at CI against my 1.85. In the changed kernel it did not act, since VectorE was waiting for Ln; in 5 it cost 0.86, and the difference for b2p 0.3 more. CI came at 21.13 there, where I had 21.1, but for another reason: 2.0 by idx and 1.1 by exclusion, less about 1.2 of compares saved. The agreement is chance. Without exclusion I had CI at 18.83; in 9 it was 19.14, 0.3 later, as Ln was.

**CI to x1, 6.65.** 7.57 to 7.60 in every version of the changed kernel with xb on GpSimd. The first hW_hi started 1.2 behind degve, where I had 1.1. The one-hot between the two hW_lo took 1.30 beside GpSimd's and moved the second one by 1.23, not 0.7: I had taken a row in which GpSimd did something else. Small terms make the other 0.4: the scales, the first hW_hi (0.84 from its start to that of hW_lo, not 0.7) and the two last products (0.69 against 0.55). hYlo isn't among them: VectorE waited 0.51 for hW_hi behind it.

**"The rest, at nothing".** 1.2 and 1.3 us more between x1 and MA0 (1 and 5). 0.6 to 0.7 is the bias product, which I priced by its columns, at most 0.1; on 64 rows of fp32r it took 0.43 in place of 0.23. 0.64 is left in 7, where VectorE's second pair of one-hots took 2.40 beside GpSimd's, in place of 1.54: what VectorE does was counted, what GpSimd does at that moment was not. 17, with the pair at 1.47, has runs 0.4 to 0.5 below 9; the rest isn't taken apart.

**Loop and tail carried over.** Right with the bias product in bf16 (32.63 in 7 against 32.64); 0.4 to 0.5 longer with fp32r (5 and 1), which stands in each pass.

**The four ScalarE tiles.** I had a gain of 0.4 at CI without exclusion. Alone they gave 0.8 (11); in 9, where Ln ended at 15.0 against 14.3 in 11, only 0.1.

In sum, of the 4.1 us between the spans of before and 5: 1.9 at CI (idx 2.0, exclusion 1.1, compares -1.2), 0.5 to x1 (one-hot 1.2, xb's move -0.7), 1.3 to MA0 (bias product 0.7, one-hots and what goes with them 0.6), 0.4 in the loop (bias product). This splitting is an estimate from the starts in the table. Single runs of the changed kernel have 0.3 to 6 us beyond 5 (76.3 to 82.3). In the two that have traces, 76.29 and 79.89, it is TensorE's rate. In the others that isn't shown: the mean granted clocks go from 0.999 down to 0.92, but the run at 82.31 has 0.955.

## What to carry to other kernels

Before a load is put ahead on an idle queue, ask which small load on another queue the first instruction waits for: here that one came 2 us later, and everything behind it. A moved instruction is priced by what the other engines do at its new place. Two changes that hide each other (idx and xb here) show next to nothing when one is undone. Bring out the parts one by one: the one that pays may stand alone.

## What the runs showed of the hardware

- GpSimd's two-operand add from SBUF held a VectorE compare with two SBUF operands until its end (in 8, 2.17 of its 2.63 us); a VectorE instruction with one operand in PSUM ran beside it at its usual 1.47. A compare with one tensor operand beside GpSimd's one-hot was not held but slowed: 1.30 in place of 0.74, with GpSimd's at 3.06 as before (3.05).
- A product of constants on 64 rows in fp32r took 0.43 us for 512 columns, whether its operand was repeated, written out or halved; on 128 rows, half of them zero, it took 0.23.
- TensorE's products can run at half rate (eight in 1.89 in place of 1.04) in a stretch where the granted clock reads 1.00, behind a wait of 1.8 us (1). A wait of 0.71 us in mid-kernel was followed by 3 to 3.5 us at the 1.2 GHz level in the traces of 10 and 17. One of 0.70 at the same place in 9 was not, nor was the wait filled with useless products in 16.
